# Flamingo block on one core: the steady tile's small operations dealt anew among VectorE and GpSimd, four tap diagonals kept, two convolutions moved

## The chip, the cores and the metric

The kernel runs on 1 core of a Trainium2 chip. The time is device microseconds of one execution, as a median of runs; one further execution was profiled. Engines are named as in the profile: PE is TensorE, DVE VectorE, ACT ScalarE, POOL GpSimd, SP SyncE (here it only issues DMAs).

## The reference, cut to what matters

```python
# x (4,512,512), ctx (4,512,256); everything float32
x = x + tanh(g_xattn) * mamba(ctx, z=layernorm(x))
x = x + tanh(g_ffn) * ffn(layernorm(x))

# mamba, channels e = 512, states n = 16, time l = 512
xc = in_proj @ ctx ;  u = silu(causal_conv(xc, 4 taps) + conv_b)
dt_lo, Bm, Cm = split(x_proj @ u) ;  delta = softplus(dt_proj @ dt_lo + b)
state = state * exp(delta * A) + (delta * u) * Bm     # scan over l
y = (sum_n state * Cm + D * u) * silu(z)

# ffn, every linear layer is:
#   rows rmsnormed, times g, scaled to 127/max|row|, rounded   (activations)
#   round(tanh(w / mean|w|)) * arctanh(mean|w|)                (weights: -1, 0, 1)
h = silu(linear(x, w1)) * linear(x, w2)               # 512 -> 2048
out = linear(h, w3)                                   # 2048 -> 512
```

## The kernel before, in words

The work is cut into 16 **tiles** k = 0 to 15: batch b = k // 4 and channel block et = k % 4 (128 channels, all 512 times). A tile has four **steps** q = 0 to 3; step s = 4k + q scans 32 channels, whose 16 states lie as 4 rows of states on 4 partition groups. Per step DVE does two halves, each one product with B (`add_input`, L1129, out of and into PSUM) and one scan (`scan`, L1138, 128x1024). ACT makes the decays (`exps`, L874), PE spreads delta times u over the partitions (`bcast_du`, L1484), POOL multiplies the scanned states with C (`times_c`, L668 or in halves L663, 128x2048 in all), and PE sums the states of two steps (`sum_states`, L1497). Once a tile DVE multiplies the finished y with silu(z) (`gated_y`, L1260), PE transposes it (`transpose_yz`, L1580) and DVE adds it to x (`add_scan`, L1165).

The ffn of earlier rows runs in the same loop. In tile k, f = k - 4 is the row tile (128 rows) that is normalised and goes through w1 and w2, and g = k - 5 the one whose hidden row of 2048 goes through w3. For g, POOL multiplies gate and up in two halves (`times_up`, L632) and both with the gain g3 (`h_gain`, L625); DVE takes the maxima (`hidden_max`, L1277); POOL takes the power -1/2 of the sum of squares (`hidden_rms`, L637 and L639); DVE makes the scale (`hidden_scales`, L1296 to L1298); ACT quantises (`quant_hidden`, L929), PE transposes (L1561) and multiplies (`down`, L1606). For f with f % 4 not 0, ACT sums the row (`row_stats`), DVE scales the variance (`row_var`, L1182), POOL takes its power (`row_rstd`, L653), DVE makes the bias (`row_bias`, L1189), ACT normalises, POOL multiplies with the gains (`mul_gains`), DVE makes the scales (`quant_scales`, `dequant_scales`, L1198 to L1211), ACT quantises, PE transposes (L1588) and multiplies with both weights (`gate_up`, L1519), and ACT takes gate and up out of PSUM (L884, L892).

Five tiles ahead, PE projects ctx (`in_proj`, m = k + 5) and convolves it as four products with diagonal matrices (`convolve`, L1465, for m from 6 on). POOL builds these diagonals in one buffer each time (`diag_taps`, L677).

Every engine runs its own list in order; the order is written out by hand, and semaphores are the only link. PE's results of one kind or another share 4 PSUM banks in a fixed order (`ring_order`); a job waits until the fourth job before it was read. PE also does matmuls that nobody reads, to keep its clock up (`keep_clock`, L1569): 10 ahead of the hidden row's transposes, 4 ahead of `down`, 4 ahead of some transposes of y.

In tiles 2 to 4 (steps 7 to 18) the ternary weights are made beside all this: POOL scales a chunk (L700), PE transposes it (L1422), ACT takes the sign. Tile 15 is followed by a tail without scans.

Of the kernel before, what the change touches and what calls it, by code (L numbers as in the profile page):

```python
# [69 lines left out]

def ring_order():
# [7 lines left out]
    for k in range(KQ):  # L79
        b, et = divmod(k, ET)  # L80
        f, g = k - LAG_F, k - LAG_G
        for q in range(Q):
# [6 lines left out]
            if q == 1:  # L89
                if sizes_due(k):  # L90
                    jobs += [("dt", k + 1), ("dt", k + 2)]
                pair = [("yzT", k - 1)] if k >= 1 else []
                if k >= 1 and k + AHEAD < KQ:
                    pair.insert(0 if conv_first(k) else len(pair), ("conv", k + AHEAD))
                jobs += pair
# [35 lines left out]
def flamingo_block(nc, x, ctx_in, g_xattn, g_ffn, in_proj_w, conv_w, conv_b, x_proj_w, dt_proj_w, dt_proj_b,  # L131
                   A_log, D_skip, w1, g1, w2, g2, w3, g3, out):
    scratch = nc.dram_tensor("bc_scratch", [B, 2 * NS, L], F32).ap()
    with ExitStack() as ctx:
# [425 lines left out]
        def _(pool):  # L560
# [25 lines left out]
            link(g.memset(sel_s[:, :], 0.0))  # L586
            for lo in range(4):
                link(g.affine_select(out=sel_s[:, :], in_=sel_s[:, :], compare_op=ALU.not_equal, fill=1.0,
                                     base=-32 * lo, pattern=[[-1, 32]], channel_multiplier=1))
# [1113 lines left out]
```

## Time and profile before

| | us |
|---|---|
| median of 3 runs | 718.19 (714.82 to 718.72) |
| the profiled execution | 720.12 |
| its span in the profile | 718.1 |
| busy PE / DVE / ACT / POOL | 619.6 / 607.9 / 558.4 / 548.3 |

The start takes until about 41 us (the first scan), the tiles until 643.7 us (the last `gated_y`), the tail the rest. A row of the profile names the line of the kernel, the engine, what is written and read, how many instructions, and in square brackets how long the engine had stood still and who ended that.

### The profile page before, as it was taken

The numbers are of one execution on the slowest core, as the hardware profiler recorded it, in microseconds if no ns is written. First come the engines' busy times: TensorE is split into PE (matmuls) and PEld (weight loads), VectorE is DVE, ScalarE is ACT, GpSimd is POOL, SyncE is SP. The second block draws the span as 40 slices with busy tenths as digits, with TensorE's granted clock in tenths as the row PEclk, the third lists the DMA queues.
The fourth block names the chain that finished last, engine by engine and source line by source line (L and its number), as shares of the span: only waits on it lengthen the run. The fifth ranks groups of instructions, "written<-read, shape, count | busy, mean of one in ns | idle before, by whom it ended". The sixth has DMA issues, their size and how long they took to land.

```text
span 718.1 us, 8217 instructions
## 1 busy us (share of the span) xinstructions
PE 619.6 (86%) x2538; PEld 248.4 (35%) x2538; DVE 607.9 (85%) x620; ACT 558.4 (78%) x805; POOL 548.3 (76%) x316
## 2 busy tenths in 40 slices
PE   6736765999869999999989999998897979796997
PEld 3311221544343333334333434332333323233443
DVE  2979959899967899987989899999999989877665
ACT  3647885689679997896879997989698969557873
POOL 2055549987598989897889999999899897967732
PEclk9865887999879999989999999999897979798999
DMA  8599873548922122233411212154111111000000
GB/s 220 168 257 330 287 269 91 165 148 231 297 86 74 44 59 74 59 81 83 93 28 53 52 47 56 46 120 102 49 55 45 45 44 45 15 16 0 16 31 29
DMA packets 40570, 72.01 MB, mean 100 GB/s; under 512 B 10912, under 2 KB 13472, under 8 KB 38352
## 3 DMA queue, kind: packets, MB, share of 16 engines
q1 hardware_dynamic: 37312, 62.07, 30.7%
q10 hardware_dynamic: 3216, 9.44, 3.9%
q8 instruction: 20, 0.33, 0.2%
q14 instruction: 22, 0.18, 0.1%
HBM read 50.51 MB, written 4.46 MB: 77 GB/s over the span
## 4 chain that ended last, share of the span: by engine, by line
PE 44%; DVE 17%; POOL 16%; issue 7%; DMA 7%; ACT 6%; SPq 2%; DVEq 0%; POOLq 0%; ACTq 0%
PE ring L1519 13%; DVE hb L1138 8%; PE y_ps L1497 7%; PE ring L1606 6%; POOL hb L668 6%; DVE dbu_ps L1129 5%; PE du_ps L1484 4%; POOL up_sb L625 4%; PE ring L1569 3%; POOL h L632 3%; DMA dl_rep<-delta 3%; DMA bc_rep<-bc_scratch 2%; PE ring L1446 2%; PE ring L1465 2%; PE ring L1456 2%
## 5 line engine op out<-in xcount | busy, mean ns | idle before, releaser
L1138 DVE TENSOR_TENSOR_SCAN hb<-dA,dbu_ps 128x1024 f32<-128x1024 f32 x128 | 292.4, 2284 | 13.5 <-ACT dA L874 4.6
L668 POOL TENSOR_TENSOR hb<-hb,bc_rep 128x2048 f32<-128x2048 f32 x52 | 235.8, 4537 | 46.7 <-DVE hb L1138 38.8
L874 ACT ACTIVATE dA<-dl_rep,a_neg 128x511 f32<-128x511 f32 x252 | 160.9, 714 | 18.9 <-DMA dl_rep<-delta 18.7
L1129 DVE TENSOR_TENSOR dbu_ps<-du_ps,bc_rep 128x1024 f32<-128x1024 f32 x128 | 157.6, 1231 | 18.5 <-PE du_ps L1484 8.2
L1497 PE MATMUL y_ps<-hb,sel_s 128*32 128x512 f32 x512 | 125.7, 636 | 2.2 <-POOL hb L668 2.2
L1484 PE MATMUL du_ps<-du,sel_q 32*128 32x512 f32 x128 | 79.9, 706 | 46.9 <-DVE dbu_ps L1129 46.5
L632 POOL TENSOR_TENSOR h<-h,up_sb 128x1024 f32<-128x1024 f32 x24 | 56.5, 2353 | 19.8 <-ACT up_sb L892 19.3
L1606 PE MATMUL ring<-w3T,hT 128*128 128x512 fp8e4 x256 | 61.5, 387 | 1.5 <-ACT hT L959 1.1
L663 POOL TENSOR_TENSOR hb<-hb,bc_rep 128x1024 f32<-128x1024 f32 x22 | 51.8, 2357 | 11.9 <-DVE hb L1138 11.6
L1497 PEld LDWEIGHTS y_ps<-hb,sel_s 128*32 128x32 f32 x512 | 28.5, 116 | 87.2 <-issue 81.5
L625 POOL TENSOR_TENSOR up_sb<-h,g3b 128x1024 f32<-128x1024 f32 x24 | 56.4, 2373 | 0.1
L1519 PE MATMUL ring<-w1T,a12T 128*128 128x512 fp8e4 x208 | 54.7, 386 | 1.9 <-ACT a12T L936 1.1
L1519 PE MATMUL ring<-w2T,a12T 128*128 128x512 fp8e4 x208 | 54.4, 384 | 0.0
L929 ACT ACTIVATE up_sb<-up_sb,h_sc 128x1024 f32<-128x1024 f32 x31 | 33.9, 1140 | 25.6 <-DVE h_sc L1298 25.6
L1569 PE MATMUL ring<-w1T,a12T 128*128 128x512 fp8e4 x178 | 48.6, 416 | 0.0
L1484 PEld LDWEIGHTS du_ps<-du,sel_q 32*128 32x128 f32 x128 | 20.5, 199 | 77.0 <-issue 76.5
L884 ACT ACTIVATE h<-ring,deq 128x512 f32<-128x512 f32 x48 | 32.7, 682 | 12.1 <-PE ring L1519 11.9
L1277 DVE TENSOR_REDUCE h_max<-up_sb 128x1 f32<-128x1024 f32 x32 | 38.1, 1210 | 1.8 <-POOL up_sb L625 1.8
L892 ACT ACTIVATE up_sb<-ring,deq 128x512 f32<-128x512 f32 x48 | 32.9, 685 | 7.3 <-PE ring L1519 7.3
L1465 PE MATMUL ring<-u,diag_w 128*128 128x512 f32 (+3 forms) x80 | 38.4, 626 | 0.0
L1446 PE MATMUL ring<-ctxT,w_inT 128*128 128x512 f32 x64 | 36.3, 708 | 2.3 <-ACT ctxT L779 2.3
L959 ACT ACTIVATE hT<-ring 128x1024 bf16<-128x1024 f16 x27 | 26.4, 1018 | 14.3 <-PE ring L1561 13.8
(174 smaller groups left out, 950.6 us busy)
## 6 DMA issues: line engine op xcount, KB each, us to landing
dl_rep<-delta SPq DMA_DIRECT2D x252, 64.0 KB, 2.0
bc_rep<-bc_scratch SPq DMA_DIRECT2D x32, 256.0 KB, 5.2
h<-in_L_ffn_w_dram SPq DMA_DIRECT2D x5, 1024.0 KB, 8.5
x<-in_L_ffn_w_dram SPq DMA_DIRECT2D x5, 1024.0 KB, 7.3
up_sb<-in_L_ffn_w_dram SPq DMA_DIRECT2D x5, 1024.0 KB, 7.9
xt<-in_x_dram SPq DMA_DIRECT2D x16, 256.0 KB, 3.1
out_dram<-x SPq DMA_DIRECT2D x16, 256.0 KB, 2.0
h<-in_L_ffn_w_dram ACTq DMA_DIRECT2D x3, 1024.0 KB, 6.1
```

The lines of the kernel that those rows point to most:

```text
L625: g.tensor_tensor(gained(ft)[:, half], hidden(ft)[:, half], g3b[:, half], ALU.mult).then_inc(h_mul, 1)
L632: g.tensor_tensor(h[:, half], h[:, half], up_sb[:, half], ALU.mult).then_inc(h_pool, 1)
L668: g.tensor_tensor(hb[:, s % 4, :, :], hb[:, s % 4, :, :], c_rep(s // 16), ALU.mult)\
L874: ins = a.activation(dA[:, s % 2, i, 1:L], dl[:, 1:L], ACT.Exp, scale=a_neg[:, s % 16, i:i + 1])
L1129: v.tensor_tensor(dbu_ps[:, :, :], du_ps[:, :].unsqueeze(1).to_broadcast([P, 2, L]), b_rep(b)[:, 2 * half:2 * half + 2, :], ALU.mult).then ...
L1138: v.tensor_tensor_scan(hb[:, s % 4, 2 * half:2 * half + 2, :].rearrange("p a l -> p (a l)"), dA[:, s % 2, 2 * half:2 * half + 2, :].rearra ...
L1465: ins = mm(dst[:, shift:L], diag_w[:, DC - 1 - shift, :], u[:, m % UB, 0:L - shift], start=(shift == 0), stop=(shift == DC - 1))
L1484: mm(du_ps[:, :], sel_q[rows, :], du[rows, k % 2, :], start=True, stop=True).then_inc(du_bc, 1)
L1497: ins = mm(y_ps[32 * q:32 * q + 32, :], sel_s[:, :], hb[:, s % 4, i, :], start=False, stop=(i == NH - 1))
L1519: ins = mm(dst[:, :], rows_T(ft)[:, m, t, :], w[:, t, 512 * c:512 * (c + 1)], start=(t == 0), stop=(t == ET - 1))
L1569: mm(dst[:, :], rows_T(ft)[:, t % 2, t // 2 % ET, :], w1T[:, t % ET, 0:512], start=True, stop=True)
L1606: ins = mm(dst[:, :], hT[:, t, :], w3T[:, t, :], start=(t == 0), stop=(t == H // P - 1))
```

## The change

POOL: `hidden_rms` comes ahead of the tile's first product with C, not behind it; the gain of the hidden row's first half comes between the two `times_up`; variance, power and bias of a row (f % 4 not 0) are three linked POOL operations (`row_affine`); the dequantising factors are one POOL operation; the four sets of tap diagonals are built once at the start and kept. DVE: the first `hidden_max` and, in tiles with et not 0, `add_scan` stand between a product with B and its scan; `hidden_scales` stands ahead of the scan. PE, ACT: no convolution in tiles with et = 3, two in those with et = 0; the 10 clock matmuls are left out where et = 3 and in tile 8. `sel_s` is gone (`sel_q` has the same columns), some early tensors lie in `hT`, and a junk output is FP8.

```diff
-def conv_first(k):
-    return k >= LEARLY and k % ET != ET - 1
+def early_convs(k):
+    if k < LEARLY or k % ET == ET - 1:
+        return []
+    m = k + AHEAD - (k % ET == 0)
+    return [m] if m < KQ else []
+
+def late_convs(k):
+    if k < 1 or k % ET == ET - 1:
+        return []
+    if k % ET == 0:
+        m = [k + AHEAD] if k >= LEARLY else [k + AHEAD - 1, k + AHEAD]
+    else:
+        m = [k + AHEAD] if k < LEARLY else []
+    return [i for i in m if i < KQ]
...
+            def row_affine(ft):
...
+                link(g.tensor_scalar(col[:, 0:1], fmv[:, ft % 4, 1:2], (1.0 + RMS_EPS) / D, RMS_EPS * LN_EPS,
+                                     ALU.mult, ALU.add))
+                link(g.tensor_tensor(col[:, 1:2], col[:, 0:1], half_neg[:, :], ALU.pow))
+                g.tensor_tensor(col[:, 2:3], fmv[:, ft % 4, 0:1], col[:, 1:2], ALU.mult).then_inc(fbias, 1)
+
+            def dequant_scales(ft):
+                pool.wait_ge(a_scale, ft + 1)
...
+                g.tensor_tensor(deq[:, ft % 4, :], am[:, :], alpha[:, 0:2], ALU.mult).then_inc(deq_done, 2)
...
+            for et in range(ET):
+                diag_taps(et)
             z_affine()
...
                         times_up(gt, 0)
+                        h_gain(gt, 0)
                         times_up(gt, 1)
                         if f % ET:
-                            row_rstd(f)
-                        h_gain(gt, 0)
+                            row_affine(f)
                         h_gain(gt, 1)
-                    if q == 2 and k + 1 + AHEAD < KQ:
-                        diag_taps(k + 1 + AHEAD)
+                        hidden_rms(gt)
+                    if q == 2 and f >= 0:
+                        dequant_scales(f)
...
+                if 1 <= ft <= TAIL:
+                    dve.wait_ge(deq_done, 2 * ft)
...
             def transpose_hidden(ft):
-                if ft < KQ - LAG_G or ft == NT - 1:
+                k = ft + LAG_G
+                spare = k < KQ and k % ET != ET - 1 and not late_convs(k)
+                if spare or ft == NT - 1:
                     keep_clock(("hT", ft, 0), ft, FILL[1] if ft < NT - 1 else LAST_FILL)
```

DVE in tile 11, from its second step's first product with B to the third step's first scan. Before:

```order
L1129 TENSOR_TENSOR dbu_ps<-du_ps,bc_rep 128x1024 [waits scan_done,du_bc]
L1138 SCALAR_TENSOR_TENSOR hb<-dA,dbu_ps 128x1024 [waits dbu_done,sum_done,exp_done]
L1129 TENSOR_TENSOR dbu_ps<-du_ps,bc_rep 128x1024 [waits scan_done]
L1277 TENSOR_REDUCE h_max<-up_sb 128x1 [waits h_mul] x2
L1189 TENSOR_SCALAR fsc<-fmv,fsc 128x1 [waits frstd]
L1260 TENSOR_TENSOR yz<-y_ps,xt 128x512 [waits ring_full0,z_done,sum_done]
L1138 SCALAR_TENSOR_TENSOR hb<-dA,dbu_ps 128x1024 [waits dbu_done,exp_done]
L1296 TENSOR_SCALAR h_sc<-h_pow,h_max 128x1 [waits h_rstd,dve_seq]
L1297 TENSOR_SCALAR h_sc<-h_sc,h_max 128x1 [waits dve_seq]
L1298 RECIPROCAL h_sc<-h_sc 128x1 [waits dve_seq]
L1165 SCALAR_TENSOR_TENSOR x<-ring,gates,x 128x4x128 [waits ring_full0]
L1129 TENSOR_TENSOR dbu_ps<-du_ps,bc_rep 128x1024 [waits scan_done,du_bc]
```

The same stretch in the changed kernel:

```order
L1164 TENSOR_TENSOR dbu_ps<-du_ps,bc_rep 128x1024 [waits scan_done,du_bc]
L1311 TENSOR_REDUCE h_max<-up_sb 128x1 [waits h_mul]
L1173 SCALAR_TENSOR_TENSOR hb<-dA,dbu_ps 128x1024 [waits dbu_done,sum_done,exp_done]
L1164 TENSOR_TENSOR dbu_ps<-du_ps,bc_rep 128x1024 [waits scan_done]
L1311 TENSOR_REDUCE h_max<-up_sb 128x1 [waits h_mul]
L1294 TENSOR_TENSOR yz<-y_ps,xt 128x512 [waits ring_full0,z_done,sum_done]
L1330 TENSOR_SCALAR h_sc<-h_pow,h_max 128x1 [waits h_rstd,dve_seq]
L1331 TENSOR_SCALAR h_sc<-h_sc,h_max 128x1 [waits dve_seq]
L1332 RECIPROCAL h_sc<-h_sc 128x1 [waits dve_seq]
L1173 SCALAR_TENSOR_TENSOR hb<-dA,dbu_ps 128x1024 [waits dbu_done,exp_done]
L1164 TENSOR_TENSOR dbu_ps<-du_ps,bc_rep 128x1024 [waits scan_done,du_bc]
L1200 SCALAR_TENSOR_TENSOR x<-ring,gates,x 128x4x128 [waits ring_full0]
```

The scale of the hidden row (`h_sc`) is made ahead of the step's second scan, the first maximum stands ahead of the first, and x's addition behind the next product.

POOL in tile 11, first from the two products of gate and up to the product with C, before and then after:

```order
L632 TENSOR_TENSOR h<-h,up_sb 128x1024 [waits up_done,silu_done] x2
L653 TENSOR_TENSOR fsc<-fsc,half_neg 128x1 [waits fvar]
L625 TENSOR_TENSOR up_sb<-h,g3b 128x1024 [waits h_pool] x2
L668 TENSOR_TENSOR hb<-hb,bc_rep 128x2048 [waits scan_done]
L637 TENSOR_SCALAR h_ss<-h_ss 128x1 [waits hss_done]
L639 TENSOR_TENSOR h_pow<-h_ss,halves 128x2 [waits h_scale,pool_seq]
```

```order
L646 TENSOR_TENSOR h<-h,up_sb 128x1024 [waits up_done,silu_done]
L639 TENSOR_TENSOR up_sb<-h,g3b 128x1024 [waits h_pool]
L646 TENSOR_TENSOR h<-h,up_sb 128x1024 [waits up_done,silu_done]
L675 TENSOR_SCALAR fsc<-fmv 128x1 [waits row_square,xn_done]
L677 TENSOR_TENSOR fsc<-fsc,half_neg 128x1 [waits pool_seq]
L678 TENSOR_TENSOR fsc<-fmv,fsc 128x1 [waits pool_seq]
L639 TENSOR_TENSOR up_sb<-h,g3b 128x1024 [waits h_pool]
L651 TENSOR_SCALAR h_ss<-h_ss 128x1 [waits hss_done]
L653 TENSOR_TENSOR h_pow<-h_ss,halves 128x2 [waits h_scale,pool_seq]
L703 TENSOR_TENSOR hb<-hb,bc_rep 128x2048 [waits scan_done]
```

The power of the hidden row (`h_pow`) and the row's bias (`fsc`) are made ahead of the product with C (`hb`).

PE in tile 8 of the changed kernel, from the convolution to the hidden row's transposes; `diag_w` rows are a convolution, `w1T` rows are read by nobody:

```order
L1495 MATMUL ring<-u,diag_w 128x509
L1601 MATMUL ring<-w1T,a12T 128x512 [waits silu_done]
L1601 MATMUL ring<-w1T,a12T 128x512 x3
L1612 MATMUL ring<-ident,yz 128x128 [waits yz_done]
L1612 MATMUL ring<-ident,yz 128x128 x3
L1514 MATMUL du_ps<-du,sel_q 128x512 [waits dbu_done,du_done]
L1539 MATMUL y_ps<-u,diag_d 128x512 [waits u_done,yz_done]
L1495 MATMUL ring<-u,diag_w 128x512 [waits up_done,tap_diag,tap_done]
L1495 MATMUL ring<-u,diag_w 128x511
L1495 MATMUL ring<-u,diag_w 128x510
L1495 MATMUL ring<-u,diag_w 128x509
L1593 MATMUL ring<-ident,up_sb 128x128 [waits tap_done,h_quant]
```

A second convolution stands where 10 clock matmuls stood; tile 7 has lost its convolution and these 10.

## Rows read from the trace of the kernel before

**Rows 1.** The page: busy time and share of each engine.
```profile
PE 619.6 (86%) x2538; PEld 248.4 (35%) x2538; DVE 607.9 (85%) x620; ACT 558.4 (78%) x805; POOL 548.3 (76%) x316
```

**Rows 2.** Windows, tiles 4, 7, 10, 13: length; busy, instructions; granted clock; DMA.
```profile
193.00:239.90 46.90, 39.67 (x169) 19.69 (x170) 34.58 (x33) 39.03 (x63) 38.59 (x18) 0.89 0.31 87
...
314.90:356.10 41.20, 41.20 (x155) 15.88 (x156) 34.28 (x31) 32.86 (x46) 33.22 (x17) 0.92 0.40 96
...
432.20:468.70 36.50, 34.61 (x150) 12.86 (x148) 34.40 (x34) 31.34 (x47) 33.17 (x17) 1.00 0.18 52
...
542.20:579.50 37.30, 32.36 (x136) 12.10 (x136) 34.47 (x34) 32.62 (x47) 33.01 (x17) 0.87 0.16 43
```

**Rows 3.** Waits: engine, line, who ended it; total us, times, longest.
```profile
DVE h_sc L1296 <- POOL h_pow L639: 13.8, 11, 1.6
...
DVE dbu_ps L1129 <- PE du_ps L1484: 8.2, 4, 3.8
```

**Rows 4.** Timeline of DVE in tile 10: start, us, line, operation, idle before.
```profile
429.86 2.33 DVE L1277 TENSOR_REDUCE h_max<-up_sb 128x1 f32<-128x1024 f32 x2
432.12 0.20 DVE L1189 TENSOR_SCALAR fsc<-fmv,fsc 128x1 f32<-128x1 f32 x1
...
432.83 2.28 DVE L1138 TENSOR_TENSOR_SCAN hb<-dA,dbu_ps 128x1024 f32<-128x1024 f32 x1
436.16 0.21 DVE L1296 TENSOR_SCALAR h_sc<-h_pow,h_max 128x1 f32<-128x1 f32 x1 [1.05 <-POOL h_pow L639]
...
437.39 1.22 DVE L1129 TENSOR_TENSOR dbu_ps<-du_ps,bc_rep 128x1024 f32<-128x1024 f32 x1
```

**Rows 5.** Timeline of POOL in tile 10.
```profile
419.91 2.35 POOL L632 TENSOR_TENSOR h<-h,up_sb 128x1024 f32<-128x1024 f32 x1
422.93 2.35 POOL L632 TENSOR_TENSOR h<-h,up_sb 128x1024 f32<-128x1024 f32 x1 [0.67 <-ACT up_sb L892]
425.24 0.55 POOL L653 TENSOR_TENSOR fsc<-fsc,half_neg 128x1 f32<-128x1 f32 x1
...
430.42 4.55 POOL L668 TENSOR_TENSOR hb<-hb,bc_rep 128x2048 f32<-128x2048 f32 x1
434.94 0.31 POOL L637 TENSOR_SCALAR h_ss<-h_ss 128x1 f32<-128x1 f32 x1
435.33 0.72 POOL L639 TENSOR_TENSOR h_pow<-h_ss,halves 128x2 f32<-128x2 f32 x1
```

**Rows 6.** Timeline of PE and DVE in tile 7.
```profile
320.63 5.63 PE L1465 MATMUL ring<-u,diag_w 128*128 128x512 f32 x8
326.09 2.32 PE L1569 MATMUL ring<-w1T,a12T 128*128 128x512 fp8e4 x10
...
332.12 1.23 DVE L1129 TENSOR_TENSOR dbu_ps<-du_ps,bc_rep 128x1024 f32<-128x1024 f32 x1 [3.13 <-PE du_ps L1484]
```

**Rows 7.** Timeline of POOL, DVE and PE in tile 13.
```profile
533.27 2.36 POOL L632 TENSOR_TENSOR h<-h,up_sb 128x1024 f32<-128x1024 f32 x1 [1.04 <-ACT up_sb L892]
...
542.21 0.68 DVE L1260 TENSOR_TENSOR yz<-y_ps,xt 128x512 f32<-128x512 f32 x1
...
543.03 1.09 PE L1580 MATMUL ring<-ident,yz 128*128 128x128 f32 x4 [3.82 <-DVE yz L1260]
...
547.92 3.36 PE L1569 MATMUL ring<-w1T,a12T 128*128 128x512 fp8e4 x10
```

**Rows 8.** Timeline of DVE and POOL in tile 4.
```profile
205.18 0.21 DVE L1189 TENSOR_SCALAR fsc<-fmv,fsc 128x1 f32<-128x1 f32 x1 [6.32 <-POOL fsc L653]
...
215.35 1.03 POOL L677 TENSOR_TENSOR diag_w<-ident,conv_col 128x512 f32<-128x512 f32 x1
...
224.07 1.23 DVE L1129 TENSOR_TENSOR dbu_ps<-du_ps,bc_rep 128x1024 f32<-128x1024 f32 x1 [3.79 <-PE du_ps L1484]
```

**Rows 9.** Timeline in tile 3: POOL scales weights, DVE makes the mask.
```profile
151.04 1.98 POOL L700 TENSOR_SCALAR up_sb<-up_sb,w_inv 128x2048 f32<-128x2048 f32 x1
...
151.38 1.66 DVE L1245 TENSOR_SCALAR at_mask<-wm 128x3 uint32<-128x3 f32 x1
```

More of the change, by code:

```diff
@@ L91, in ring_order @@
                     jobs += [("dt", k + 1), ("dt", k + 2)]
[L92 to L95, printed above, removed]
+                jobs += [("conv", m) for m in early_convs(k)]
+                if k >= 1:
+                    jobs.append(("yzT", k - 1))
+                jobs += [("conv", m) for m in late_convs(k)]
             if q == 2 and g >= 0:
@@ L585, in _ @@
                 g.memset(dA[:, j, :, 0:1], 0.0).then_inc(masks, 1)
[L586 to L589, printed above, removed]
             for j in range(8):
@@ L823, in row_stats @@
                     act.wait_ge(row_square, n_sum - 1)
-                a.activation(z_junk[:, :], row, ACT.Copy, scale=-1.0 / D, accum_out=fmv[:, ft % 4, 0:1]).then_inc(row_mean, 1)
+                a.activation(z_junk[:, :], row, ACT.Copy, scale=-1.0 / D, accum_out=fmv[:, ft % 4, 0:1], saturate=False).then_inc(row_mean, 1)
                 act.wait_ge(row_mean, n_sum)
-                a.activation(z_junk[:, :], row, ACT.Square, bias=fmv[:, ft % 4, 0:1], accum_out=fmv[:, ft % 4, 1:2])\
+                a.activation(z_junk[:, :], row, ACT.Square, bias=fmv[:, ft % 4, 0:1], accum_out=fmv[:, ft % 4, 1:2], saturate=False)\
                  .then_inc(row_square, 1)
@@ L993, in _ @@
                             step_sizes(k + 1)
-                        if k + AHEAD < KQ and conv_first(k):
-                            conv_evac(k + AHEAD)
+                        for m in early_convs(k):
+                            conv_evac(m)
                         if f >= 0 and f % ET:
@@ L999, in _ @@
                             quant_hidden(g)
-                        if 1 <= k < KQ - AHEAD and not conv_first(k):
-                            conv_evac(k + AHEAD)
+                        for m in late_convs(k):
+                            conv_evac(m)
                     if q == 2 and f >= 0:
@@ L1021, in _ @@
                             silu_u(ET)
-                        if k + AHEAD < KQ:
-                            silu_u(k + AHEAD)
+                            silu_u(AHEAD)
+                        for m in early_convs(k) + late_convs(k):
+                            silu_u(m)
                         if f >= 0:
@@ L1321, in _ @@
                             row_bias(f)
+                        if k >= 1 and et:
+                            add_scan(k - 1)
                     scan(s, 0)
@@ L1326, in _ @@
                     if q == 1 and g >= 0:
[L1327 removed]
                         top = hidden_max(g, 1)
[L1329 to L1332 removed]
                     if q == 1 and k >= 1:
                         gated_y(k - 1)
+                    if q == 1 and g >= 0:
+                        after(top)
+                        hidden_scales(g)
                     if q == 2:
@@ L1343, in _ @@
                     if q == 1:
-                        if g >= 0:
-                            after(top)
-                            hidden_scales(g)
-                        if k >= 1:
+                        if k >= 1 and et == 0:
                             add_scan(k - 1)
@@ L1557, in transpose_hidden @@
                         pe.wait_ge(h_quant, 2 * ft + j + 1)
-                    if j or KQ - LAG_G <= ft < NT - 1:
+                    if j or not (spare or ft == NT - 1):
                         take(("hT", ft, j))
@@ L1627, in _ @@
                                 dt_proj(k + 1 + t)
-                        if k < KQ - AHEAD and conv_first(k):
-                            convolve(k + AHEAD)
+                        for m in early_convs(k):
+                            convolve(m)
                         if k >= 1:
@@ L1633, in _ @@
                         skip_term(k)
-                        if 1 <= k < KQ - AHEAD and not conv_first(k):
-                            convolve(k + AHEAD)
+                        for m in late_convs(k):
+                            convolve(m)
                     if q == 2:
```

66 lines of the change are left out of this document (32 added, 34 removed).

## The prediction

> **What bounds the kernel now.** I read the page first: PE and DVE are both busy 85% or so, and no engine is full [rows 1], so the limit is a loop through several engines. The windows from one `gated_y` (the product of y with silu(z)) to the next say how long a tile is: 36.50 us in tile 10, 41.20 in tile 7, 46.90 in tile 4, 37.30 in tile 13 [rows 2]. In tile 10 DVE is busy 34.40 of 36.50. Each tile holds eight products with B and eight scans, and DVE cannot drop one of those. So there DVE sets the pace, and what it stands still or does besides is what can be won. The list of waits says where it stands still: 13.8 us in 11 tiles for POOL's power of the hidden row, 8.2 us in four places for PE's spreading of delta times u [rows 3]. The timelines of single tiles then say why.
>
> Tile 10: the maxima end at 432.2, the scan at 435.1, and DVE then waits 1.05 us for the power [rows 4]. POOL has it ready only at 436.05 because a product with C of 4.55 us stands ahead of it, from 430.42 [rows 5]. POOL in turn stood still 0.67 us between its two products of gate and up, for ACT.
>
> **The ordinary tile (5, 6, 9, 10, 11).** I lay tile 10 out anew from the same start; each link between engines costs about 0.1 us.
> POOL: first product of gate and up 419.91 to 422.25; first gain, of 2.35, to 424.6 (this fills the pause); second product to 427.0; the row's three operations. Of these the trace shows 0.55 for a power and 0.31 for a scalar operation [rows 5], so with a second small one and two links about 1.3, where 0.52 stood: to 428.3. Second gain to 430.65; power of the hidden row, 0.31 + 0.72 and a link, to 431.75; product with C to 436.3.
> DVE: the first maximum (1.13 of the 2.33 for two) moves between a product with B and its scan. These are linked, so 0.2 us of it hides; it is free at 427.3, when the gain (424.6) is long there. The second maximum waits for the gain at 430.65 and ends at 431.9, `gated_y` 432.5 (before 432.83), the scale, three linked operations of about 0.2, 433.1, scan to 435.45, next product with B at 435.5 instead of 437.39 [rows 4]. That is 1.9 won; 0.45 goes back because `add_scan`, 0.65 long, now stands behind that product (0.2 hidden). About 1.4 us stays. The bias and the two factors that leave DVE hardly count: they stood in the linked gaps.
> Can the others follow? PE's spreading for 435.5 is done at 434.7, PE's `down` waited for DVE anyway, and POOL's last half product with C follows the scan. POOL's next tile begins at 455.0 instead of 456.3. Its own additions, 0.8 for the row and 0.25 for the factors, stand against the 0.67 pause and 1.03 us of a diagonal [rows 5, 8] (up to tile 9), and it waited for DVE over 1 us later in the tile. So POOL is close to full, but still carries it. I take -1.4 for tiles 5 and 6 and -1.3 for 9, 10 and 11, whose PE has less to spare: **-6.7**. From below: nothing but the pause, -0.3 each. From above: wait, pause and hidden parts, -2.1 each.
>
> **Tile 7.** PE does the convolution in 5.63 us, partly at half clock, and then ten clock matmuls of 2.32, and only then the hidden row's transposes; so DVE waits 3.13 us at 332.12 [rows 6] and 0.96 once more. Both blocks go. The transposes then wait for ACT (322), `down` begins near 323, and its spreading is due at about 325, when DVE, 1.25 us early, does not need it yet. The product with B at 332.12 comes at 327.7, the next tile's first at 335.6, and `gated_y` of tile 8 six us earlier. Here -6 (bounds -3, if ACT or the clock takes it back, and -7).
>
> **Tile 8** gets the second convolution, 3.65 us at full clock, for 2.2 us of clock matmuls. ACT takes this convolution out ahead of normalising row tile 4, so POOL's gains wait some 4 us and DVE about 3 us. That eats what the early power wins: -0.6 (bounds +2 and -2).
>
> **Tile 4** takes over tile 3's convolution. DVE stands still 6.32 us there for POOL, which came late from a DMA wait, so PE has the time. But ACT's normalising falls behind both convolutions and a weight chunk: from 205.4 to about 207.9. The gains, the product with C and the scaling of the last weight chunk follow 2.4 later. PE needs that chunk before the sums and `gate_up`, and DVE waits on the latter already, 3.79 us at 224.07 [rows 8]. The diagonal's 1.03 us, gone from POOL just there, gives part back, and PE, idle less, may keep its clock. I take +2 (bounds 0 and +3.5).
>
> **Tiles 1 to 3** lose a convolution and 1.03 us of POOL work each, where DVE is nearly full: only `add_scan`'s hidden 0.2 each, -0.8 with PE's small lateness (bounds 0, -3). The four diagonals at the start lie inside POOL's long wait for the statistics of z: 0.
>
> **Tiles 12 to 14** have no convolution, and PE stands still before `gated_y`, 3.82 us in tile 13. Then the granted clock is at its lower level, 1.2 GHz: ten clock matmuls take 3.36 us where they took 2.32 at 2.4 GHz [rows 6, 7]; the window's mean is 0.87 [rows 2]. Transpose, spreading, skip term and these ten take 8.1 instead of 4.8 us and stand on the path: PE, not DVE, sets the pace. Of the change only the stretch before `gated_y` helps: before, 8.94 us from POOL's second product to `gated_y` [rows 7]; now that product starts 1.25 after ACT's last up part instead of 0.1, and then takes 2.35 + 1.3 + 2.35 + 0.1 + 1.13. That is 8.4 against 9.1. With the even share of DVE about -0.6 each: **-1.8** (bounds 0; -6 if the clock stays up). **Tile 15** has no clock matmuls before the transposes and a PE that is busy from the transpose of y to the end: -1.3 (0, -2.5).
>
> **The sum:** -0.8 + 2 - 2.8 (5, 6) - 6 - 0.6 - 3.9 (9 to 11) - 1.8 - 1.3 = -15.2. Against the profiled execution, 720.12, this is 704.9. The median of the runs is 1.9 lower than it, so I write 704.0. The tail is unchanged. All ends together: -31 and about 0.
>
> **A rule that speaks against it.** In tile 3 DVE's mask of 3 columns took 1.66 us, where such an operation takes 0.2; it began beside POOL's weight scaling and ended with it [rows 9]. Now the scale of the hidden row stands beside the product with C. But DVE's bias, of the same form, took 0.20 at 432.12 while exactly that product ran [rows 4, 5].
> The Trainium skill (SBUF — State Buffer, section "SBUF: two separate sides") says that DVE and GpSimd share one pair of ports under an exclusive lock, and that the loser stands still for the other's whole instruction, if the DVE operation is in a two-port mode or has two SBUF inputs. By that rule the mask agrees, the bias does not.
>
> **Rivals.**
> *The block:* the three scale operations wait for the end of the product with C. They start 0.9 us after it, so some 3.6 us of its 4.55 are lost, less the 1.4 won, in 11 tiles: +24, about 744 less the other wins, 735. The bias row speaks against it. 2%.
> *The clock falls into the long part (the slow side):* tiles 7, 8, 11 and 15 lose ten clock matmuls each. If PE then drops to 1.2 GHz in `down`, the sums and `gate_up`, each drop costs what it costs in tile 13, 8.1 - 4.8 = 3.3 us, now on the path. It needs 15.2 + 3.6 = 18.8 us, six tiles with one such drop more, to end above 721.8; it would then be about 724. For it: tile 11 keeps only 4 of the fill matmuls and its PE will wait some 2 us for ACT. Against: in tiles 7 and 8 PE is solid. 5%.
> *GpSimd becomes the bound:* if its small operations cost more than their rows, or tiles 4 and 8 lose their upper bounds, half of the gain is left, about 711. POOL is within 1 us of full in the new order. 15%.
> *The clock recovers:* a shorter pause before `gated_y` keeps PE at 2.4 GHz, and tiles 12 to 14 win 2.1 instead of 0.6 each: 700. 15%. The pause only falls from 3.8 to about 3.3, so I don't count on it.
> *The change does nothing:* the wait moves from the power to the second maximum, which waits for the gain behind `row_affine`. I find 0 to 0.9 us of such a wait, less than the one removed; were it all of it, only tile 7 would be left, 714 to 716. 3%.
> The forecast: 60%.
>
> **The numbers.** 704.0 us; the range 698 to 712 takes in the recovering clock and most of the POOL case. Half a per cent, 3.6 us, is about what a measurement of this kernel can tell. Faster by more: 0.60 + 0.15 + 0.15 and half of the last case, 0.91; within, the other half: 0.02; slower: 0.02 + 0.05 = 0.07.
>
> **What will show it.** Right: no wait of `h_sc` for `h_pow`; tiles of about 35 us from 9 to 11 and tile 7 under 36; DVE's wait at 332 gone; tile 4 longer by about 2 with the wait at its end grown; in tiles 12 to 14 a new DVE wait for `du_ps` of about 1 us and a clock still near 0.87. Wrong: long `h_sc` rows (the block), slow `down` or `gate_up` rows in tiles 11 or 15 (the clock), POOL without pauses and DVE waiting for `up_sb` or `a` in every tile (POOL).

## The result, and the profile after

| | before | after |
|---|---|---|
| median | 717.51 us (714.82 to 718.72, 4 runs) | 708.7 us (706.8 to 711.93, 4 runs) |
| the profiled execution | 720.12 | 706.8 |
| its span | 718.1 | 705.0 |

The ratio is 0.9897, 95% interval 0.9854 to 0.9941: 8.8 us faster in the medians. 704.0 was forecast, with a range of 698 to 712. The sum of the steps was 15.2 us, and the two profiled executions differ by 13.3.

The page after, to set against [rows 1]: every engine keeps nearly all of its work (PE gives up 6.8 us, the others 1.3 to 2.4), and the span shrinks round it.

```profile
PE 612.8 (87%) x2498; PEld 246.9 (35%) x2498; DVE 605.5 (86%) x578; ACT 556.0 (79%) x805; POOL 547.0 (78%) x335
```

The windows after, from `gated_y` to `gated_y`, of tiles 4, 7, 8, 10, 11 and 13, with the columns of [rows 2].

```profile
193.11:240.37 47.26, 42.50 (x176) 20.60 (x175) 34.24 (x29) 39.34 (x64) 37.82 (x21) 0.93 0.30 85
312.80:347.73 34.93, 32.64 (x137) 12.26 (x138) 33.84 (x28) 32.16 (x44) 33.26 (x17) 1.00 0.48 114
347.73:385.80 38.07, 35.82 (x147) 13.76 (x146) 35.09 (x34) 31.66 (x48) 32.97 (x21) 1.00 0.19 49
421.56:456.46 34.90, 34.29 (x150) 12.87 (x149) 33.84 (x29) 30.00 (x46) 33.62 (x20) 1.00 0.20 53
456.46:492.72 36.26, 30.68 (x129) 11.32 (x127) 33.84 (x30) 31.45 (x43) 33.05 (x17) 0.90 0.46 109
530.47:568.16 37.69, 33.23 (x136) 12.31 (x136) 33.94 (x30) 32.95 (x48) 33.68 (x20) 0.86 0.16 42
```

Tile 10 went from 36.4 us to 34.90 with DVE busy 33.84 of it, so about 1 us is left to win there. Tile 7 went from 41.14 to 34.93. But tile 11 stayed at 36.26, with the granted clock at 0.90, and tile 13 got longer, from 37.3 to 37.69, with the clock at 0.86.

The lengths of the tiles in all profiles of this study, in us, each from its `gated_y` to the next, in groups of tiles ("start-3" is all up to the `gated_y` that opens tile 4, "tail" what follows the last one; the names below the first four are those of the experiments):

```
              start-3   4     5-6     7      8    9-10   11   12-14   15   tail   span
before         193.0  46.8   75.1   41.1   39.2   73.4  36.3  111.9  26.8  74.4  718.1
before, again  192.6  45.6   75.1   39.5   40.9   73.4  36.3  112.5  26.9  74.5  717.1
after          193.1  47.3   72.4   34.9   38.1   70.7  36.3  113.0  25.2  74.1  705.0
after, again   191.8  49.7   72.9   35.6   38.1   70.7  36.3  113.0  25.2  74.1  707.4
power_only     192.1  44.4   72.2   37.8   36.5   70.7  35.2  112.6  26.9  74.5  702.9
deal_only      193.6  49.5   74.8   35.6   38.7   72.8  36.7  111.3  27.2  74.7  715.0
conv_back      193.7  42.8   72.9   36.8   36.2   70.7  36.2  110.3  27.2  74.6  701.3
fill11         191.3  48.6   72.9   34.9   38.6   70.7  35.3  110.8  27.2  74.6  705.0
late_fill      191.4  49.5   72.9   34.9   38.6   70.7  36.2  106.3  24.0  74.6  699.2
power_late     193.7  45.3   72.2   39.5   36.5   70.8  35.2  107.4  24.0  74.1  698.7
best_a         191.4  46.8   72.4   34.9   38.0   70.7  36.2  106.3  24.0  74.8  695.5
best_b         191.9  44.0   72.9   36.8   36.2   70.7  35.3  106.3  24.0  74.5  692.6
conv8_back     196.4  46.2   72.9   34.9   38.7   70.7  36.3  113.0  25.2  74.1  708.4
```

The ordinary tile is what the forecast laid out. DVE and then POOL after, at the place of [rows 4, 5]:

```profile
420.44 1.21 DVE L1311 TENSOR_REDUCE h_max<-up_sb 128x1 f32<-128x1024 f32 x1
421.56 0.68 DVE L1294 TENSOR_TENSOR yz<-y_ps,xt 128x512 f32<-128x512 f32 x1
422.16 0.20 DVE L1330 TENSOR_SCALAR h_sc<-h_pow,h_max 128x1 f32<-128x1 f32 x1
...
422.73 2.28 DVE L1173 TENSOR_TENSOR_SCAN hb<-dA,dbu_ps 128x1024 f32<-128x1024 f32 x1
425.12 1.23 DVE L1164 TENSOR_TENSOR dbu_ps<-du_ps,bc_rep 128x1024 f32<-128x1024 f32 x1
```

```profile
414.31 2.38 POOL L646 TENSOR_TENSOR h<-h,up_sb 128x1024 f32<-128x1024 f32 x1
416.78 0.19 POOL L675 TENSOR_SCALAR fsc<-fmv 128x1 f32<-128x1 f32 x1
417.06 0.55 POOL L677 TENSOR_TENSOR fsc<-fsc,half_neg 128x1 f32<-128x1 f32 x1
...
420.67 0.72 POOL L653 TENSOR_TENSOR h_pow<-h_ss,halves 128x2 f32<-128x2 f32 x1
421.37 4.54 POOL L703 TENSOR_TENSOR hb<-hb,bc_rep 128x2048 f32<-128x2048 f32 x1
```

The power is ready at 421.4, before DVE asks for it at 422.16; where a wait of 1.05 us stood, no bracket stands. The three scale operations take 0.16 to 0.21 us beside the product with C from 421.37: nothing is blocked. The Trainium skill (SBUF — State Buffer, section "SBUF: two separate sides") has an exclusive lock on the ports that DVE and GpSimd share; these rows agree with it only if this one-column operation does not contend for them. The next product with B comes 3.56 us after `gated_y`, where it took 5.2.

The waits after, which answer to [rows 3]: the wait for the power is gone from the list, the one for PE's spreading has grown from 8.2 us in 4 places to 12.2 in 15, and the one for POOL's gain (1.8 us before) is now 5.1.

```profile
DVE dbu_ps L1164 <- PE du_ps L1514: 12.2, 15, 2.8
...
DVE h_max L1311 <- POOL up_sb L639: 5.1, 6, 1.2
```

### The profile page after: what moved, and what is told of

Its sections match the earlier page's. It is cut to its first block, busy times and chain, and to the rows that moved or that the text cites. A ratio compares the mean times of both kernels' runs of the same rounds, so it can differ in the third digit from the quotient of the medians.

```text
span 705.0 us, 8139 instructions
## 1 busy us (share of the span) xinstructions
PE 612.8 (87%) x2498; PEld 246.9 (35%) x2498; DVE 605.5 (86%) x578; ACT 556.0 (79%) x805; POOL 547.0 (78%) x335
## 4 chain that ended last, share of the span: by engine, by line
PE 31%; DVE 19%; ACT 7%; issue 7%; POOL 6%; DVEq 0%; ACTq 0%; POOLq 0%
DVE hb L1173 11%; PE ring L1549 7%; PE ring L1638 5%; PE y_ps L1527 5%; DVE dbu_ps L1164 4%; PE ring L1601 4%; PE du_ps L1514 3%; POOL h L646 3%; ACT dA L908 2%; PE ring L1593 2%; POOL up_sb L639 2%; PE ring L1495 2%; PE y_ps L1539 1%; DVE am L1232 1%; PE ring L1612 1%
## 5 line engine op out<-in xcount | busy, mean ns | idle before, releaser
L1164 DVE TENSOR_TENSOR dbu_ps<-du_ps,bc_rep 128x1024 f32<-128x1024 f32 x128 | 157.8, 1233 | 23.0 <-PE du_ps L1514 12.2
L1527 PE MATMUL y_ps<-hb,sel_q 128*32 128x512 f32 x512 | 126.2, 639 | 4.1 <-POOL hb L703 4.1
L1527 PEld LDWEIGHTS y_ps<-hb,sel_q 128*32 128x32 f32 x512 | 28.6, 116 | 87.9 <-issue 81.0
L1549 PE MATMUL ring<-w1T,a12T 128*128 128x512 fp8e4 x208 | 54.4, 385 | 1.9 <-ACT a12T L970 1.1
L918 ACT ACTIVATE h<-ring,deq 128x512 f32<-128x512 f32 x48 | 32.7, 681 | 11.4 <-PE ring L1549 10.9
L1601 PE MATMUL ring<-w1T,a12T 128*128 128x512 fp8e4 x138 | 41.3, 444 | 0.0
L963 ACT ACTIVATE up_sb<-up_sb,h_sc 128x1024 f32<-128x1024 f32 x31 | 33.8, 1138 | 4.2 <-DVE h_sc L1332 4.2
L1638 PEld LDWEIGHTS ring<-w3T,hT 128*128 128x128 bf16 x256 | 23.8, 99 | 37.9 <-issue 10.8
```

The costliest lines, as they stand in the source:

```text
L1164: v.tensor_tensor(dbu_ps[:, :, :], du_ps[:, :].unsqueeze(1).to_broadcast([P, 2, L]), b_rep(b)[:, 2 * half:2 * half + 2, :], ALU.mult).then ...
L1527: ins = mm(y_ps[32 * q:32 * q + 32, :], sel_q[:, 0:32], hb[:, s % 4, i, :], start=False, stop=(i == NH - 1))
L1549: ins = mm(dst[:, :], rows_T(ft)[:, m, t, :], w[:, t, 512 * c:512 * (c + 1)], start=(t == 0), stop=(t == ET - 1))
L1601: mm(dst[:, :], rows_T(ft)[:, t % 2, t // 2 % ET, :], w1T[:, t % ET, 0:512], start=True, stop=True)
L1638: ins = mm(dst[:, :], hT[:, t, :], w3T[:, t, :], start=(t == 0), stop=(t == H // P - 1))
```

## Experiments

The first series was to share the gain out over the change's parts and to find what held tiles 11 to 14.

**power_only**: the kernel before, with the power alone moved ahead of the first product with C.

```diff
                         h_gain(gt, 0)
                         h_gain(gt, 1)
+                        hidden_rms(gt)
...
                     if q == 1:
-                        if gt >= 0:
-                            hidden_rms(gt)
```

> The kernel before with one thing moved: GpSimd takes the power of the hidden row ahead of the tile's first product with C; nothing on VectorE or PE is moved. Theory: VectorE's wait for the power (1.0 to 1.6 us in 11 tiles) goes and this is most of what the ordinary tiles win: tiles 5, 6, 9 and 10 about 1 us shorter each, tile 7 none or little (PE sets it), tiles 12 to 14 none (half clock), in all 4 to 6 us shorter than before. Rival: GpSimd is the bound, so the product with C and all behind it come 1 us later and VectorE waits elsewhere: under 1 us in all, and the gain of the change comes from the dealing of VectorE's work and the first gain in GpSimd's pause.

Measured: 708.48 us (704.71 to 710.65), ratio 0.9894 (0.9833 to 0.9955). One moved pair of instructions gives what the whole change gives, and more than the 4 to 6 us expected (9.2 in the medians, 7.6 by the ratio). DVE in tile 10 of its profile, at the place of [rows 4]:

```profile
418.48 0.68 DVE L1259 TENSOR_TENSOR yz<-y_ps,xt 128x512 f32<-128x512 f32 x1
419.08 2.28 DVE L1137 TENSOR_TENSOR_SCAN hb<-dA,dbu_ps 128x1024 f32<-128x1024 f32 x1
421.27 0.19 DVE L1295 TENSOR_SCALAR h_sc<-h_pow,h_max 128x1 f32<-128x1 f32 x1
```

The scale comes straight after the scan, without a bracket. In the table, tiles 5 to 11 are 252.4 us in all, as after (252.3), against 265.1 before. The second profiles of the same code in these tiles, power_late and after2, have 254.2 and 253.6. The distribution differs: after is 2.9 us shorter in tile 7, and longer by 1.5 in tile 8, 1.1 in tile 11 and 0.2 in the others together. So a theory by which the power is only a part, and the dealing the larger one, is out for these tiles.

**deal_only**: the changed kernel with the power back behind the product, and the scale back behind the scan.

```diff
-                        hidden_rms(gt)
...
                     if q == 1:
+                        if gt >= 0:
+                            hidden_rms(gt)
...
```

> The changed kernel without its first part: the power of the hidden row is again behind the tile's first product with C, and the scale of the hidden row again behind the scan; all else stays. Theory (the power's move is the gain in the ordinary tiles, the rest carries nothing there): VectorE waits 1.0 to 2.5 us for the power again, tiles 5, 6, 9 and 10 are 36 to 38 us, tile 7 36 to 37, in all 716 us or within 4 of the kernel before. Rival (each part is enough by itself, the loop has one slack to give): tiles 9 and 10 under 35.7, in all under 711.

Measured: 714.99 us (710.81 to 716.84, 10 runs), ratio 0.9969 (0.9939 to 1.0). As long as the power is late, all the other parts together are worth little. The wait is back as the list of waits shows (first fence), and tile 10 as DVE's timeline shows (second):

```profile
DVE h_sc L1331 <- POOL h_pow L653: 15.5, 11, 1.8
```

```profile
429.24 2.27 DVE L1174 TENSOR_TENSOR_SCAN hb<-dA,dbu_ps 128x1024 f32<-128x1024 f32 x1
433.07 0.21 DVE L1331 TENSOR_SCALAR h_sc<-h_pow,h_max 128x1 f32<-128x1 f32 x1 [1.56 <-POOL h_pow L653]
```

What the dealing took off DVE comes back as a longer wait (1.56, was 1.05): DVE is early, POOL is not. Tiles 5, 6 and 8 to 11 are only 1.0 us shorter in all than in the first profile before (223.0 against 224.0; 2.6 shorter than in the second), and most of what it wins is in tile 7 (35.6 against 41.1 and 39.5).

**conv_back**: the changed kernel with the convolutions and clock matmuls in the old places on PE; the four kept diagonals stay.

```diff
-                spare = k < KQ and k % ET != ET - 1 and not late_convs(k)
+                spare = k < KQ
```
`early_convs` and `late_convs` are written so that together they return [k + AHEAD], at the place where it stood before.

> The changed kernel with the convolutions and the 10 clock matmuls where they were before (one convolution in every tile, late where et is 3, clock matmuls in all). Theory: tile 7 goes back from 34.9 us to 39.5 to 41, tile 8 from 38.1 to 37 or so, tile 4 from 47.3 to 46.8 or less, tile 11 from 36.3 to 35: in all 3 to 5 us longer than the changed kernel. Rival (tile 7's gain is the power's and the first maximum's, and PE would have kept up): tile 7 under 37, in all no longer than the changed kernel.

Measured: 707.32 us (703.37 to 709.46), ratio 0.9861 (0.9803 to 0.992). Moving the convolutions and leaving out clock matmuls, which this run takes back together, is worth nothing that can be measured; 3 to 5 us were expected. Its windows of tiles 7 and 8:

```profile
309.40:346.23 36.83, 36.83 (x152) 14.37 (x153) 33.85 (x29) 31.83 (x44) 32.08 (x17) 1.00 0.43 105
346.23:382.41 36.18, 35.40 (x151) 13.61 (x150) 35.10 (x33) 32.01 (x49) 34.19 (x21) 1.00 0.20 55
```

Together 73.0 us, as after (34.93 + 38.07): what tile 7 wins, tile 8 pays. POOL shows where, in tile 8 after:

```profile
357.05 1.27 POOL L627 TENSOR_TENSOR a<-a,g1b 128x512 f32<-128x512 f32 x1 [3.47 <-ACT a L936]
```

ACT takes out the second convolution first, POOL stands still 3.47 us for the normalised row (4 was forecast), and DVE then 1.89 (3 was forecast).

Tile 11 stayed at 36.2, though the ten clock matmuls stand in it again. PE's rows there show that the clock fell ahead of them, in the skip term, and PE had not stood still since 443.88:

```profile
456.13 2.08 PE L1530 MATMUL y_ps<-u,diag_d 128*128 128x512 f32 x2
458.00 4.20 PE L1592 MATMUL ring<-w1T,a12T 128*128 128x512 fp8e4 x10
```

At full speed they take 1.12 and 2.32 us, as the next run shows.

**fill11**: the changed kernel with the ten clock matmuls back in tiles 11 and 15.

```diff
-                spare = k < KQ and k % ET != ET - 1 and not late_convs(k)
+                spare = k < KQ and (k in (11, 15) or k % ET != ET - 1) and not late_convs(k)
```

> The changed kernel with the 10 clock matmuls ahead of the hidden row's transposes back in tiles 11 and 15. Theory: without them PE waits 2.65 us in tile 11, its clock falls, and the transposes, the start of the down product and what follows run at half clock; with them tile 11 falls from 36.3 us to about 35.0, while tile 15, whose PE is busy anyway and at half clock, gets 0 to 2 us longer: together -1.3 to +1. Rival (tile 11 is held by VectorE's own work): tile 11 unchanged, 0 to +2 in all.

Measured: 707.18 us (706.82 to 708.43), ratio 0.9869 (0.982 to 0.9918); the total does not tell it from after, the tiles of its one profile do. PE in tile 11, first after, then in fill11:

```profile
458.96 1.12 PE L1539 MATMUL y_ps<-u,diag_d 128*128 128x512 f32 x2
462.73 2.07 PE L1593 MATMUL ring<-ident,up_sb 128*128 128x128 f16 x16 [2.65 <-ACT up_sb L963]
464.59 1.91 PE L1601 MATMUL ring<-w1T,a12T 128*128 128x512 fp8e4 x4
```

```profile
459.56 1.12 PE L1539 MATMUL y_ps<-u,diag_d 128*128 128x512 f32 x2
460.52 2.32 PE L1601 MATMUL ring<-w1T,a12T 128*128 128x512 fp8e4 x10
463.34 0.62 PE L1593 MATMUL ring<-ident,up_sb 128*128 128x128 f16 x8 [0.49 <-ACT up_sb L963]
464.38 0.62 PE L1593 MATMUL ring<-ident,up_sb 128*128 128x128 f16 x8 [0.42 <-ACT up_sb L963]
464.84 1.03 PE L1601 MATMUL ring<-w1T,a12T 128*128 128x512 fp8e4 x4
```

Without the ten, PE stands still 2.65 us, and then the four fp8 matmuls take 1.91 us where they take 1.03 in fill11. Its windows of tiles 11 and 13:

```profile
457.06:492.35 35.29, 30.29 (x139) 11.15 (x137) 33.85 (x30) 32.11 (x44) 34.25 (x17) 1.00 0.48 116
528.85:565.92 37.07, 32.62 (x136) 12.16 (x136) 33.94 (x30) 32.94 (x48) 33.67 (x20) 0.87 0.17 43
```

Tile 11 is 1.0 us shorter. That is not certain to come from the ten: of the four profiles in which the changed order has them in tile 11, fill11 and best_b have 35.3 us there, conv_back and best_a 36.2, as without them.

Tiles 12 to 14 are 110.8 in all instead of 113.0 (110.3 in conv_back), and PE's ten clock matmuls of tile 12 show how, first after, then in fill11:

```profile
498.37 4.35 PE L1601 MATMUL ring<-w1T,a12T 128*128 128x512 fp8e4 x10
```

```profile
498.00 3.12 PE L1601 MATMUL ring<-w1T,a12T 128*128 128x512 fp8e4 x10
```

After, the clock comes back only when they are over; in fill11 it comes back among them. From the transposes of y to those of the hidden row PE takes 9.10, 8.95 and 8.94 us in tiles 12, 13 and 14 after, and 7.87, 8.33 and 8.63 in fill11: 2.2 us less, all that the three tiles differ by. Tile 15 becomes 2.0 longer by its ten matmuls: leaving them out was right there.

**late_fill**: the changed kernel, with 14 clock matmuls where none stood, or 18 where 4 stood, ahead of y's transposes from tile 12 on, where PE stood still.

```diff
+                if f >= 1 and 12 <= k + 1 < KQ:
+                    dst, done = keep_clock(("yzT", k), f - 1, 14 if sizes_due(k + 1) else 18)
-                if f >= 1 and k + 1 < KQ and not sizes_due(k + 1):
+                elif f >= 1 and k + 1 < KQ and not sizes_due(k + 1):
```

> The changed kernel with 14 clock matmuls (18 in even tiles, where 4 stood) put ahead of the transpose of y in tiles 12 to 15, into the 3.5 to 4.4 us in which PE stands still there. Theory: the pause lets the granted clock fall to 1.2 GHz, and the half clock on the path from the transpose of y to the hidden row's transposes sets the pace of these tiles. Then the clock stays at 2.4 GHz, the tiles 12 to 14 fall from 37.7 us to 35.2 to 35.8, tile 15 by about 1, and the whole is 6 to 9 us shorter than the changed kernel. Rival (VectorE or GpSimd sets the pace there, the clock is a bystander): the clock rises and the tiles stay at 37.5 or so, no gain. Second rival: the fill does not hold the clock, and 14 matmuls at half clock (6 us) outlast the pause: tiles 2 us longer each.

Measured: 699.31 us (696.48 to 702.15), ratio 0.9756 (0.9697 to 0.9815). PE in tile 13, first after, then in late_fill, against [rows 7]:

```profile
531.29 1.09 PE L1612 MATMUL ring<-ident,yz 128*128 128x128 f32 x4 [3.51 <-DVE yz L1294]
532.31 2.07 PE L1514 MATMUL du_ps<-du,sel_q 32*128 32x512 f32 x2
```

```profile
527.74 3.19 PE L1601 MATMUL ring<-w1T,a12T 128*128 128x512 fp8e4 x14
531.18 0.65 PE L1614 MATMUL ring<-ident,yz 128*128 128x128 f32 x4 [0.25 <-DVE yz L1294]
531.77 1.12 PE L1514 MATMUL du_ps<-du,sel_q 32*128 32x512 f32 x2
533.78 2.32 PE L1601 MATMUL ring<-w1T,a12T 128*128 128x512 fp8e4 x10
```

The window of tile 13 in late_fill:

```profile
530.44:565.34 34.90, 32.95 (x153) 12.43 (x150) 33.84 (x29) 33.02 (x49) 33.69 (x20) 1.00 0.17 46
```

The clock stays at 2.4 GHz (1.00), the spreading takes 1.12 us instead of 2.07, and the tile is as long as tile 10 was. Tiles 12 to 14 are 106.3 instead of 113.0, tile 15 is 24.0 instead of 25.2, and the medians differ by 9.4 us. So it was PE at 1.2 GHz, not DVE and not POOL, that set the late tiles. The Trainium skill (TensorE: Matmul & The Clock Gate, "Part 1: The HAM clock gate") says that half speed is the default and that activity lifts it; this fence agrees with its 1.12 us, but the fall in tile 11 of conv_back, without a pause, is not explained by that sentence.

The second series asked whether the one gain comes on top of the other, and whether the dealing shows once PE is out of the way.

**power_late**: power_only with late_fill's edit.

> The kernel before with two things only: the power of the hidden row ahead of the product with C, and the 14 or 18 clock matmuls ahead of the transpose of y in tiles 12 to 15. Theory (the power and the clock are all, the rest of the change is worth nothing): tiles 5 to 11 sum to 252.5 us as in the change and in the power alone, tiles 12 to 14 fall from 37.2 to 37.7 us to 35.3 or so, the whole is within 2 us of the changed kernel with the late clock matmuls (699 us). Rival (the dealing of VectorE's work and the first gain in GpSimd's pause are worth 0.4 to 0.6 us a tile once PE does not hold the tile): tiles 9 to 14 are 0.4 or more longer each than there, in all 4 to 6 us longer.

Measured: 699.19 us (697.85 to 702.17), ratio 0.9752 (0.9702 to 0.9803), the same as late_fill. The power is worth 9 us, and on top of it the late clock matmuls another 9 (708.48 to 699.19); what they give to the kernel before without the power was not run. The dealing is seen by itself here: tiles 12 to 14 are 107.4 against 106.3 in late_fill (and in best_b, which like this run has the ten in tile 11), 0.37 a tile.

**best_a**: late_fill, with tile 11's ten matmuls back.

```diff
-                spare = k < KQ and k % ET != ET - 1 and not late_convs(k)
+                spare = k < KQ and (k == 11 or k % ET != ET - 1) and not late_convs(k)
```

> The changed kernel with the late clock matmuls (tiles 12 to 15) and the 10 ahead of the hidden row's transposes back in tile 11. Theory (clock on the path): tile 11 falls from 36.2 to 35.2 us, tile 12 from 36.2 to 35.5, the whole 1 to 2.5 us under the late clock matmuls alone, about 697.5. Rival: tile 12 is held by something other than the clock (row statistics on VectorE), then only tile 11 gains, 698.5.

Measured: 704.23 us (697.28 to 706.08, 6 runs), ratio 0.9805 (0.9755 to 0.9855), where about 697.5 was expected. The profiled run is the fastest of the six, with a span of 695.5; its tiles are as short as late_fill's, so what makes the median later is not in this profile. Tile 11 stayed at 36.2 with its matmuls back: as in conv_back the clock fell ahead of them, and the ten took 4.07 us.

**best_b**: conv_back with late_fill's edit, and tile 15 alone without the ten.

```diff
-                spare = k < KQ
+                spare = k < KQ - 1
```

> The same as the run before it but with the convolutions and all clock matmuls up to tile 14 where they stood in the kernel before. Theory (moving the convolutions is worth nothing over all: tile 7 gives back 2 us, tile 8 wins 2, tile 4 wins up to 4): within 2 us of the run before it, or up to 3 shorter if tile 4 really pays for two convolutions. Rival (the convolutions' new places are worth what tile 7 shows): 2 to 5 us longer.

Measured: 699.56 us (694.44 to 705.57, 6 runs), ratio 0.9738 (0.9686 to 0.9789). Its profile has the shortest span of all, 692.6, and its ratio lies clear of the change's own. Against late_fill and power_late (0.9756, 0.9752) it can't be told apart. It is 4.7 us under best_a, more than expected, but the two intervals overlap.

**conv8_back**: the changed kernel with the convolution of m = 8 back in tile 3, so that tile 4 has only that of m = 9.

```diff
+    if k == 3:
+        return [8]
...
-        m = [k + AHEAD] if k >= LEARLY else [k + AHEAD - 1, k + AHEAD]
+        m = [k + AHEAD]
```

> The changed kernel with one convolution moved back: channel block 8's is in tile 3 again, not beside block 9's in tile 4; tiles 7 and 8 stay as changed. In nine profiles tile 4 took 48.3 us on average with both convolutions (five of them, 46.8 to 49.5) and 44.7 with one (four, 42.8 to 46.8). Theory: tile 4 pays for the pair, and falls to 43 to 46 us, tile 3 grows by under 1, in all 3 to 4 us shorter than the changed kernel. Rival (the difference is chance in the arrival of weights and of C): tile 4 stays at 47 to 49.

Measured: 709.63 us (704.49 to 712.59), ratio 0.9822 (0.9756 to 0.9887), with a before of 720.34 on that chip. Tiles 3 and 4 came to 81.65 us in all. With both convolutions in tile 4, six profiles give 79.0 to 83.6; with one in each, six others give 77.0 to 78.7. This one should have joined the second group and did not: tile 4 fell to 46.2, and tile 3 grew to 35.4 (32.1 and 33.8 after). Inconclusive.

**before2** and **after2**: the two kernels unchanged, one more profile of each.

> The kernel before once more, for a second profile. If the one before was a slow instance of its first 240 us, tile 4 is 43 to 45 us here, and tile 7 shows whether its 41.1 us belong to the kernel (theory: 39 to 41) or to a chance fall of the clock (rival: under 38).

> The changed kernel once more, for a second profile. If tiles 12 to 14 are 36.2 to 37.3 us as in two other kernels whose code is the same there, and not 37.6 to 37.8, the length of the half-clock stretch is a matter of when it falls, not of the change. Tile 4 is expected at 47 to 49.

Measured: spans of 717.1 and 707.4. From tile 5 on, most tiles repeat to 0.1 us; tile 7 does not, nor does tile 5 after, nor tiles 8, 13 and 14 before. Tile 4 does not repeat at all: 46.8 and 45.6 before, 47.3 and 49.7 after. Tiles 12 to 14 came to 113.0 again (and in conv8_back), so their length belongs to the changed kernel and is no chance of one execution.

## Why the prediction was right, and where it was not

Means of the two profiles of each kernel, against the terms of the forecast:

| term | forecast | measured |
|---|---|---|
| start to tile 3 | -0.8 | -0.4 |
| tile 4 | +2 | +2.3 |
| tiles 5, 6 | -2.8 | -2.4 |
| tile 7 | -6 | -5.1 |
| tile 8 | -0.6 | -2.0 |
| tiles 9 to 11 | -3.9 | -2.8 |
| tiles 12 to 14 | -1.8 | +0.8 |
| tile 15 | -1.3 | -1.7 |
| tail | 0 | -0.3 |
| sum | -15.2 | -11.4 |

**The ordinary tile** was right in mechanism and size: -1.5 in tile 10, -1.2 in tile 9. Tile 11 won nothing. But its working counts the filled pause and the hidden first maximum among what brings it, and by the runs they don't: the power's move alone gives 1.1 to 1.5 a tile in tiles 9 to 11 (power_only), and the dealing alone next to nothing as long as the power is late (deal_only). The lay-out followed all of them as one path and never asked what each is worth without the others.

**Tile 7** was right in its sum (-5.1; -6 was said), but not all of it is the convolution's. Its 41.1 us before were in part a chance of that execution: the granted clock there was 0.92, in the second profile 0.96 (39.5 us). The power alone has 37.8 at a clock of 1.00 and, in power_late, 39.5 at 0.96; conv_back and best_b, with the convolution in its old place, have 36.8, the change 34.9 and 35.6. The moved convolution is paid for in tile 8, as the forecast said with ACT and POOL (its 4 and 3 us measured 3.47 and 1.89). That tile 8 still won 2.0 where 0.6 was said is in part the clock, 0.96 and 0.92 before and 1.00 after, which the forecast had not counted. Tiles 7 and 8 together came to -7.1 against -6.6: that the two errors cancel is luck. What I had not asked is whether this move pays in all; conv_back answers 73.0 against 73.0.

**Tile 4** got its +2.3 in the means. The wait at its end, 3.79 in [rows 8] and 3.78 in before2, was to grow. It shrank to 2.76 in the first profile after and grew in the second:

```profile
224.56 1.23 DVE L1164 TENSOR_TENSOR dbu_ps<-du_ps,bc_rep 128x1024 f32<-128x1024 f32 x1 [2.76 <-PE du_ps L1514]
```

```profile
226.21 1.23 DVE L1164 TENSOR_TENSOR dbu_ps<-du_ps,bc_rep 128x1024 f32<-128x1024 f32 x1 [5.43 <-PE du_ps L1514]
```

Of the six profiles with both convolutions in tile 4, four have 5.13 to 5.43 us and two 2.8. But conv8_back, with one, has 5.34. So the wait grew as said in most profiles, and that the second convolution is the cause is not shown.

**The step that failed** is the term "tiles 12 to 14: -1.8", with tile 11's -1.3. The stretch ahead of `gated_y` was right: in tile 13, from the end of ACT's last up part (521.99) to `gated_y` (530.47), it is 8.48 us now where it was 9.08, and 8.4 against 9.1 was laid out. PE's pause shrank to 3.51 (3.3 said), and DVE waits up to 0.96 us for `du_ps`, as said. Yet the tiles grew. The forecast took the other stretch on the path as fixed: from PE's transposes of y to those of the hidden row, 8.1 us, with the clock coming back among the ten clock matmuls. It did not stay 8.1:

| tile | before | before2 | after | after2 | fill11 | conv_back |
|---|---|---|---|---|---|---|
| 12 | 7.98 | 8.10 | 9.10 | 9.12 | 7.87 | 7.58 |
| 13 | 8.08 | 8.43 | 8.95 | 8.96 | 8.33 | 8.18 |
| 14 | 8.26 | 8.44 | 8.94 | 8.95 | 8.63 | 8.55 |

In the first profiles that is 2.7 us more in the three tiles, and the stretches ahead of the three next `gated_y` give 1.6 back (0.60, 0.46 and 0.49; 1.8 was said): +1.1, as measured in these profiles. The ten clock matmuls that the change left out of tile 11 have a part in it: with them back, in fill11 and conv_back, the stretch has its old length, and tiles 12 to 14 are 110.8 and 110.3 where before has 111.9 and 112.5: -1.1 to -2.2, about the -1.8 that I had written. The forecast had looked at these ten only as a part of the slow rival, and held that chance to be small. They are not all of it: deal_only lacks them too and has 111.3. Why the clock comes back later stays open. So does tile 11's own 1.3: it stayed at 36.3 without the ten, and with them it was 35.3 in two profiles and 36.2 in two others.

**The rivals.** The block fell: no long `h_sc` row. GpSimd as the bound is not seen either, though the time, 708.7, lies between the forecast and this rival's 711 and alone could not tell: its three row operations measured 0.19, 0.55 and 0.19 us, DVE's wait for its gain is 5.1 us in 6 places, and late_fill won its 9.4 us with POOL's work as it was. It has little to spare: it is busy 33.62 of 34.90 us in tile 10. The recovering clock did not come by itself; late_fill forced it, and tiles 12 to 14 then came 5.6 us under the first profile before, where the rival had 6.3. The clock's fall behind a longer pause happened in tile 11, for which it was named (granted clock 0.90; 0.95 and 1.00 before). By fill11 its price is 1.0 us in it and 2.2 in the three after it; the 3.3 named were for one tile.

**The number.** The sum of steps fell short by 3.8 us, and the failed step alone by 3.7 (2.6 in tiles 12 to 14, 1.1 in 9 to 11); the other terms cancel, which is luck. The forecast also has a slip: 720.12 - 15.2 - 1.9 is 703.0, not 704.0. The median is 5.7 above 703.0. Of this 3.8 are the steps; the rest is that the medians differ by 8.8 us and the means of two profiles by 11.4, less 0.7 by which the median before came out lower (717.51 instead of 718.19).

## What to carry to other kernels

Find the one link on which the path hangs before you deal out work around it: here two instructions of 0.3 and 0.7 us, moved past one 4.5 us instruction, gave as much as the whole change, and the rest came out neutral in sum. When you take filler matmuls out of a tile, look at the rows of TensorE behind it and in the next tiles, not only at the matmuls' own 2.3 us. And an engine that stands still 3.5 us once a tile may still be the one that sets the tile, if its clock falls in that pause: filling it won as much as the whole reordering (9.4 and 8.8 us).

## What the runs showed of the hardware

A pause of 2.65 us (tile 11 after) or 3.51 us (tile 13) is followed by rows at half speed: four fp8 matmuls 1.91 instead of 1.03 us, the spreading 2.07 instead of 1.12. A pause is not needed for it: in tile 11 of conv_back PE shows none for 12 us, and the skip term took 2.08 us instead of 1.12. In tile 13 fourteen matmuls of 3.19 us in the pause, which leave 0.25 us of it, keep the granted clock at 1.00 for the whole tile. When the clock comes back differs between two kernels with the same code in a tile: the ten clock matmuls of tile 12 took 4.35 us after and 3.12 in fill11.

GpSimd's two scalar operations for a row took 0.19 us each here, less than the 0.31 of [rows 5] (that operation itself still took 0.30), so a row's variance, power and bias cost it 0.93 us busy and 1.1 from first to last.
